# Summing y over the groups in DRAM with accumulating DMAs, in a grouped MLP with layer norm and projection

## The reference

```python
xr = x.reshape(Bx, Tx, 8, LATENT)
h = jnp.einsum('btel,elf->btef', xr, W1) + b1
h = jax.nn.gelu(h, approximate=False)
y = jnp.einsum('btef,efl->btel', h, W2) + b2
y = y.reshape(Bx, Tx, Dx)
eo = jax.nn.silu(emb) @ emb_W + emb_b
scale, shift = jnp.split(eo[:, None, :], 2, axis=-1)
hn = _layernorm(y, ln_g, ln_b) * (1.0 + scale) + shift
proj = jax.nn.silu(hn) @ out_W + out_b
return x + proj
```

## Time and profile before

| | |
|---|---|
| median of 3 runs | 706.13 us |
| lowest, highest | 706.08, 706.57 us |
| the profiled execution: span from first to last instruction | 704.2 us |
| PE busy | 700.5 us (99%) |
| DVE busy | 603.7 us (86%) |
| ACT busy | 469.3 us (67%) |
| POOL busy | 104.1 us (15%) |
| granted TensorE clock, mean over the span | 0.999 |

### The profile page before, as it was taken

One profiled execution on the slowest core, in us unless ns is written; L12 is line 12 of the kernel. 1 busy time (PEld: TensorE's weight loads), 2 busy tenths in 40 slices (PEclk: granted clock), 3 DMA queues, 4 the chain that ended last, 5 costly groups with the idle time before them and its releaser, 6 DMA issues.

```text
span 704.2 us, 8302 instructions
## 1 busy us (share of the span) xinstructions
PE 700.5 (99%) x3082; PEld 577.9 (82%) x3082; DVE 603.7 (86%) x725; ACT 469.3 (67%) x526; POOL 104.1 (15%) x68
## 2 busy tenths in 40 slices
PE   9999999999999999999999999999999999999998
PEld 6888888888888888888888888888888888888887
DVE  6888999999999989899887999999999978677512
ACT  7898888888878879888883456454656454555500
POOL 0000000000000011100121332423232432322100
PEclk9999999999999999999999999999999999999999
DMA  6766557344232531332789687887699877565531
GB/s 240 247 232 207 187 203 231 109 169 150 90 121 90 209 120 61 120 107 104 210 293 301 183 279 233 275 256 246 219 293 264 256 217 210 183 176 143 156 120 60
DMA packets 51880, 133.22 MB, mean 189 GB/s; under 512 B 4096, under 2 KB 25216, under 8 KB 49408
## 3 DMA queue, kind: packets, MB, share of 16 engines
q1 hardware_dynamic: 46944, 115.79, 46.9%
q0 software_dynamic: 4608, 16.78, 12.3%
q10 hardware_dynamic: 288, 0.13, 0.1%
HBM read 82.35 MB, written 33.55 MB: 165 GB/s over the span
## 4 chain that ended last, share of the span: by engine, by line
PE 99%; DMA 0%; ACT 0%; DVE 0%; issue 0%; DVEq 0%
PE psum L949 48%; PE psum L939 25%; PE psum L923 25%; PE psum L1001 2%; DMA wraw<-in_W 0%; PE psum L971 0%; ACT W L534 0%; DVE res L901 0%; DVEq L125 0%
## 5 line engine op out<-in xcount | busy, mean ns | idle before, releaser
L665 DVE TENSOR_TENSOR g_lo<-g_raw,g_hi 128x1024 fp32r<-128x1024 f32 x128 | 158.4, 1239 | 27.9 <-ACT g_hi L495 25.3
L489 ACT ACTIVATE g_raw<-psum,cols 128x1024 f32<-128x1024 f32 x128 | 142.9, 1116 | 34.1 <-PE psum L923 24.9
L949 PE MATMUL psum<-oW_hi,s_lo 128*128 128x512 f32 x496 | 152.7, 389 | 0.0
L949 PE MATMUL psum<-oW_hi,s_hi 128*128 128x512 f32 x496 | 152.7, 389 | 0.0
L949 PE MATMUL psum<-oW_lo,s_hi 128*128 128x512 f32 x496 | 152.6, 389 | 0.0
L939 PE MATMUL psum<-g_hi,W 128*128 128x512 f32 x512 | 136.8, 389 | 0.0
L923 PE MATMUL psum<-xT_hi,W 128*128 128x512 f32 x508 | 135.8, 389 | 0.0
L939 PEld LDWEIGHTS psum<-g_hi,W 128*128 128x128 f32 x512 | 96.1, 188 | 20.0
L923 PEld LDWEIGHTS psum<-xT_hi,W 128*128 128x128 f32 x508 | 95.3, 188 | 19.8
L949 PEld LDWEIGHTS psum<-oW_hi,s_hi 128*128 128x128 f32 x496 | 93.1, 188 | 19.4
L949 PEld LDWEIGHTS psum<-oW_hi,s_lo 128*128 128x128 f32 x496 | 93.1, 188 | 19.3
(11 more groups left out here) (77 smaller groups left out, 679.8 us busy)
## 6 DMA issues: line engine op xcount, KB each, us to landing
y_scratch<-y_stage SPq DMA_DIRECT2D x32, 512.0 KB, 3.1
yb<-y_scratch SPq DMA_DIRECT2D x16, 1024.0 KB, 4.8
res<-in_x SPq DMA_DIRECT2D x32, 512.0 KB, 6.1
res<-out_b_all POOLq DMA_DIRECT2D x32, 512.0 KB, 4.5
xT_raw<-in_xT SPq DMA_DIRECT2D x31, 512.0 KB, 4.3
out<-res SPq DMA_DIRECT2D x31, 512.0 KB, 4.1
tail_cols<-in_emb_T SPq DMA_DIRECT2D x24, 512.0 KB, 7.2
wraw<-in_out_W SPq DMA_DIRECT2D x16, 256.0 KB, 4.9
```

The lines of the kernel that those rows point to most:

```text
L489: nc.scalar.activation(g_raw[:, m % 2], ring(m), ACT.Gelu, bias=cols[:, R_B1 + k:R_B1 + k + 1]).then_inc(gelu_done, 1)
L665: nc.vector.tensor_tensor(g_lo[:, m % 2], g_raw[:, m % 2], g_hi[:, m % 2].bitcast(F32), ALU.subtract).then_inc(glo_done, 1)
L949: mm = nc.tensor.matmul(proj(q)[:, half], v[:, g, cut], w[:, g, half], start=(g == 0 and k == 0), stop=(g == G - 1 and k == 2))
```

## The change

A second DRAM tensor, `y_sum`, holds the sum of y over the groups. In the first stage the four items of group 0 are stored to it by an additional plain DMA on SP's queue, right behind the store to `y_scratch`. The other 28 items are added to it by an accumulating DMA on POOL's queue (`add_y`), each of 512 KB, 1 KB per row piece, from the same `y_stage` buffer. Each of these waits for the addition before it on the same tokens. `stage_y` now also waits until the buffer's additional DMA of two items earlier has landed. The mean loads 128 x 256 of `y_sum` into `mean_total` (`load_sum`, on SP's queue), and DVE's three additions per unit are gone, 48 instructions in all.

```diff
+    y_sum = nc.dram_tensor("y_sum", [NP, P, TP], F32, kind="Internal").ap()
...
+            def load_sum(p):
+                if p >= 1:
+                    sp.wait_ge(mean_done, p)
+                sp.dma_start(mean_total[:], y_sum[p]).then_inc(sum_landed, 16)
...
                     for p in range(2):
                         load_y(p)
+                    for s in range(2):
+                        sp.wait_ge(y_summed[s], 16 * len(range(NT + s, Y0_ITEM + 1, 2)))
+                if n == 22:
+                    sp.wait_ge(emb_dot, SUMS)
+                    load_sum(0)
+                if n == 24:
+                    load_sum(1)
+                if n == 26:
+                    load_sum(2)
...
                 sp.dma_start(y_scratch[PT * t:PT * t + PT, :, g].rearrange("h p t -> p h t"),
                              y_stage[:, n % 2].rearrange("p (h t) -> p h t", h=PT)).then_inc(y_stored[n % 2], 16)
+                if g == 0:
+                    sp.dma_start(y_sum[PT * t:PT * t + PT].rearrange("h p t -> p h t"),
+                                 y_stage[:, n % 2].rearrange("p (h t) -> p h t", h=PT)).then_inc(y_set[n % 2], 16)
...
             for s in range(2):
                 sp.wait_ge(y_stored[s], 16 * (N // 2))
+                sp.wait_ge(y_summed[s], 16 * ((N - NT) // 2))
             for q in range(QN):
+                if q % 2 == 0 and q // 2 + 3 < NP:
+                    load_sum(q // 2 + 3)
...
             def mean_of(p):
-                pool.wait_ge(mean_tree, 3 * p + 3)
+                pool.wait_ge(sum_landed, 16 * (p + 1))
...
-            mean_of(0)
-            mean_of(1)
-            var_of(0)
-            var_of(1)
+            def add_y(n):
+                g, t = ORDER[n]
+                last = ITEM_OF[g - 1, t]
+                if g == 1:
+                    pool.wait_ge(y_set[last % 2], 16 * (last // 2 + 1))
+                else:
+                    pool.wait_ge(y_summed[last % 2], 16 * ((last - NT) // 2 + 1))
+                pool.wait_ge(y_staged, n + 1)
+                pool.dma_start(y_sum[PT * t:PT * t + PT].rearrange("h p t -> p h t"),
+                               y_stage[:, n % 2].rearrange("p (h t) -> p h t", h=PT), accum_op=ALU.add
+                               ).then_inc(y_summed[n % 2], 16)
+
+            for n in range(NT, N):
+                add_y(n)
+                if n == 21:
+                    mean_of(0)
+                if n == 23:
+                    mean_of(1)
+                if n == 24:
+                    var_of(0)
+                if n == 26:
+                    mean_of(2)
+                if n == 28:
+                    var_of(1)
             pool.wait_ge(out_b_landed, 16)
             for q in range(2):
                 add_bias(q)
             for i in range(NP):
-                if i + 2 < NP:
-                    mean_of(i + 2)
                 if 2 * i + 2 < QN:
                     add_bias(2 * i + 2)
+                if i + 3 < NP:
+                    mean_of(i + 3)
...
                 if n >= 2:
                     act.wait_ge(y_stored[n % 2], 16 * (n // 2))
+                    if n - 2 < NT:
+                        act.wait_ge(y_set[n % 2], 16 * (n // 2))
+                    else:
+                        act.wait_ge(y_summed[n % 2], 16 * ((n - NT) // 2))
...
-                if ahead < NP:
-                    mean_sum_first(ahead)
-                    mean_sum_rest(ahead)
```

More of the change, by code:

```diff
@@ L189, in cond_ffn_program @@
         tail_cols = [at(f"tail_cols{k}", [P, K], R0 + o * KB) for k, o in enumerate((36, 40, 80, 84, 88, 92))]
-        mean_part1 = at("mean_part1", [P, HG, TP], R0 + 124 * KB)
         yb = (yb0, yb1, yb2)
@@ L237, in cond_ffn_program @@
         y_stored = [sem(f"y_stored{s}") for s in range(2)]
+        y_set = [sem(f"y_set{s}") for s in range(2)]
+        y_summed = [sem(f"y_summed{s}") for s in range(2)]
         y_landed = [sem(f"y_landed{s}") for s in range(3)]
-        mean_tree = sem("mean_tree")
+        sum_landed = sem("sum_landed")
         mean_done = sem("mean_done")
@@ L728, in modulation, with centre @@
                     nc.vector.tensor_scalar(half_c[:], mod_c[:, 0], 0.5, None, ALU.mult).then_inc(mod_step, 1)
-            def mean_part(p):
-                return mean_part1 if p == 1 else sq
-            def mean_sum_first(p):
-                if p == 1:
-                    dve.wait_ge(emb_dot, SUMS)
-                dve.wait_ge(y_landed[p % 3], 16 * (p // 3 + 1))
-                nc.vector.tensor_tensor(mean_part(p)[:, 0:4], yb[p % 3][:, 0:4], yb[p % 3][:, 4:8], ALU.add
-                                        ).then_inc(mean_tree, 1)
-            def mean_sum_rest(p):
-                part = mean_part(p)
-                dve.wait_ge(mean_tree, 3 * p + 1)
-                nc.vector.tensor_tensor(part[:, 0:2], part[:, 0:2], part[:, 2:4], ALU.add).then_inc(mean_tree, 1)
-                dve.wait_ge(mean_tree, 3 * p + 2)
-                if p >= 1:
-                    dve.wait_ge(mean_done, p)
-                nc.vector.tensor_tensor(mean_total[:], part[:, 0], part[:, 1], ALU.add).then_inc(mean_tree, 1)
-            def centre(p, h):
+            def centre(p, h):
+                dve.wait_ge(y_landed[p % 3], 16 * (p // 3 + 1))
                 dve.wait_ge(mean_done, p + 1)
@@ L817, in _ @@
                     modulation(0, EARLY, 0)
-                if (n, c) == (21, 1):
-                    mean_sum_first(0)
-                if (n, c) == (22, 1):
-                    mean_sum_rest(0)
-                if (n, c) == (22, 2):
-                    mean_sum_first(1)
                 if (n, c) == (23, 1):
@@ L827, in _ @@
                     centre(0, 1)
-                if (n, c) == (24, 1):
-                    mean_sum_rest(1)
                 if (n, c) == (24, 2):
```

## The result

The changed kernel took 720.09 us (median of 4 runs, 719.27 to 721.66) beside 706.33 us before (706.08 to 706.57): 1.0197 times as long, with a 95% interval of 1.0183 to 1.0212, so 13.8 us slower. The forecast was slower, 711.5 us: 5.4 us where 13.8 came.

What follows compares the result with a forecast made beforehand. PE was taken as the bound, never standing still, so less DVE work gains nothing. Waits of 1.5 + 1.1 + 0.5 + 2.3 = 5.4 us on 706.13 gave 711.5 us; range 705.9 to 722, the case's own 707.2 to 716.

Steps and rivals of the forecast that it cites:

- term 0: Removing DVE's three additions per unit, some 37 us over 16 units, gains nothing, since PE is not waiting.
- The turn's path: Turn of the stages: bias additions behind add_y(31) land late, delaying finish(0), embedding columns and finish(1), so PE waits.
- Stores ahead of x: Items 0 to 3: second stores delay x; PE waits 1.5 us after item 2 and 1.1 after item 3.
- The 2 MB piece: Where a 2 MB piece comes too, engine work reaches into the next item; PE waits 0.5 us (0 to 0.7).
- Steady items: First stage: x goes before the addition, whose 3 us fit in the rest of the 10.88 us item; no loss.
- POOL's statistics: POOL's waits on mean and variance stand behind additions, but these are ready within the item: cost nothing.
- rival (b): Additions get ahead of x in 28 items, PE waits 1.4 to 1.9 us each: 746 to 759 us; chance 0.13.
- the case that I gave 0.05: Partial case of additions getting ahead of x: 716 to 725 us; chance 0.05.
- the 2.5 to 3 us that I had worked out: How much later x would land in 28 items if the additions got ahead of it.
- the signs that I had named: Among them: x lands near 4.0 to 4.5 us from item 14 on; first bias addition lands near 369.
- 6 us or more: Sign that the forecast is wrong: x lands this long after its issue in steady items.
- The turn: Turn of the stages: finish(0) moves by 5.4 us and PE waits 2.3 us (0 to 4.5).

Runs made afterwards that it cites:

- e7: The kernel before, with DVE's three additions per unit cut to one of two groups: 706.31 us, ratio 0.9997.
- e1: The changed kernel with group 0's four plain stores to y_sum issued behind the load of x and the next weights: 715.18 us, ratio 1.0141.
- e2: The changed kernel with the first two bias additions issued behind the addition of item 29, ahead of items 30 and 31: 716.76 us, ratio 1.0153.
- e14: The changed kernel with POOL's all-reduce of the mean of unit 2 moved ahead of the addition of item 26: 719.36 us, ratio 1.0187.
- e10: The changed kernel with the edits of e1 and e2 together, the additions of y issued at once: 712.05 us, ratio 1.0077.
- e6: The changed kernel with plain copies in place of the 28 accumulating DMAs, leaving the summing out: 714.56 us, ratio 1.0112.
- e5: The changed kernel with y_sum laid out for 4 KB pieces, 128 per addition instead of 512: 726.43 us, ratio 1.0281.
- e12: e10, but SP issues each load of x before it waits for y and stores it: 708.43 us, ratio 1.0029.
- e4: The changed kernel with the edits of e1, e2 and e3 together: 716.43 us, ratio 1.0133.
- e3: The changed kernel with each accumulating DMA issued only when the x loaded beside it has landed: 723.6 us, ratio 1.025.

## Why the prediction was right and wrong

**Right: the sign, and that DVE's work is worth nothing.** "So nothing that takes work off DVE can gain" was term 0; e7 measured 0.9997. The turn's path was also the right one (bias late, `finish(0)`, embedding columns, `finish(1)`, PE), and so was the place of the early loss, the x behind item 2's stores; moving each (e1, e2) took its loss away.

**Stores ahead of x: forecast 1.5 + 1.1 = 2.6, measured 5.3.** After item 2 PE waited 2.6 us against 1.5, inside the bounds of 0.4 to 3.1. After item 3 it waited nothing against 1.1: the wait before had made PE itself late. Items 0 and 1, costed at nothing, gave 1.0: the x behind item 0's two stores took 6.65 us. What the sum had no term for is the clock, 1.7 us behind this one wait. The scatter is large here: e14, in which nothing of this part is changed, loses 3.5 by item 6, with no single wait over 0.8 us. So the nearness of 1.5 and 2.6 is partly luck.

**The 2 MB piece: forecast 0.5, measured 1.1** in items 6 to 10, above the bound of 0.7. No experiment took the piece away; that it is the cause rests on the place, and e1, e2 and e10, which leave this part as it is, lost nothing from item 7 to 10.

**Steady items: forecast 0, measured 4.7 (items 23 to 31).** This is the step that failed: "By that x goes first, and the 3 us lie in the rest of the item". The first half held: the bias DMA of rows 10 had indeed come last (its first packet 5.1 us after the issue, 1.5 as a rule), and in after 81% of a load of x starts before the addition's first packet. What did not follow is that an x that goes first is undisturbed, and that was put at nothing without a row that shows it. Its packets take 274 ns instead of 186, and it lands 5.6 us after its issue in this stretch instead of 4.1. Between 70 and 230 us x takes 0.9 us more (5.3 against 4.4 in the middle), and from item 11 to 22 PE loses next to nothing. Between 230 and 340 us it takes 1.5 more and PE loses 4.7 us, in steps of 1.3, 1.4, 1.2 and 0.5 at items 25, 26, 28 and 30. That fits a number that stood in the rival, "It decides from an x that lands over 1.1 us later in steady items", but 1.1 is no sharp point: in e6 an x 0.8 us later went with 1.7 lost. The step of 1.2 is where the all-reduce stands beside `g_lo`. For this there was no term either: I had put POOL's statistics down at "nothing" since they are ready within the item, and did not ask what DVE does beside them.

So rival (b) had the late x and neither its cause nor its size, and the case that I gave 0.05, "716 to 725", holds the result. By the Trainium skill's rule that I weighed ("DMA: Bandwidth & Descriptors", section "Queues, rings and completion order"), engines going round-robin between queue rows, x would be slowed where both have packets to send. The trace has that for the last fifth of x, and e5 for longer, up to 8.5 us to landing; but most of x was slow with nothing of the addition to take turns with, and the 2.5 to 3 us that I had worked out did not come. Of the signs that I had named, x "near 4.0 to 4.5 us" failed (5.6), and so did a first bias addition near 369 (384); "6 us or more" was reached by single loads only (6.3 at most).

**The turn: forecast 2.3 (0 to 4.5), measured 4.4.** `finish(0)` came 8.6 us later against PE's own lag, where I had 5.4: `add_y(31)` took 13.8 us, not the 3 us of engine time and 2 us of way that I had put ahead of the bias. PE's wait was 2.8, the rest the clock again. So a shift of 5.8 us was hidden, more than the 4.4 to 5.4 of the working; with those, a shift of 8.6 would have made PE wait 3.2 to 4.2.

**The sum.** Of the 10.3 us missed in the profiled execution (15.7 less 5.4), the clock is 3.2, items 23 to 31 are 4.7, and the rest, 2.4, are waits of which each was forecast within about a factor of two.

**Open.** What slows the packets of x between POOL's issue and the addition's first packet is not known; it came with a copy as with an addition, and with 128 packets as with 512. Nor is it known when PE's clock falls behind a wait: in e1 PE stood 3.0 us at the turn, and the clock stayed at 1.00. A version faster than before didn't come out, and e7 says why: PE never waits for what the change saves.

## What to carry to other kernels

Work on an engine that nobody waits for costs nothing (e7), while the DMAs that replace it delayed a load with 0.85 us to spare. So before moving a sum into DMAs, find the load with the least slack and ask what is issued ahead of it, what is in flight beside it, and how much it can stretch: here 0.9 us more cost next to nothing, and 1.5 us more cost PE 3 to 5. Going first doesn't protect it. If the traffic must be there, issue the tight load earlier (e12: from 13.8 down to about 2 us with the same bytes, the two bias additions moved as well). And when costing a wait of PE of two us or more, look for a trace that shows the clock behind one.

## What was not expected of the hardware

- Two waits of PE of 2.6 and 2.8 us were each followed by a granted clock of 0.50 for 2.6 to 2.9 us, which cost 1.7 and 1.5 us. It fell too behind waits of 2.4 us in e4 (0.54 over 3 us), 2.2 in e14 and 2.0 in e5. It stayed at 1.00 behind waits of 1.9 us (e3 at 258 us, e5 at 404) and less, and also behind the one of 3.0 us in e1.
- An accumulating DMA of 512 KB from SBUF to DRAM on POOL's queue, in 1 KB pieces, landed 8.2 to 11.0 us after its issue with x beside it (150 to 330 us) and 5.9 to 7.5 as a plain copy on the same queue (e6), while a plain store of the same y on SP's queue took 3.1. At 128 packets each, adding took 8.3 us (e5, 328 ns a packet) and copying 6.2 (e6, 159 ns). In the landing the adding is the smaller part; in the kernel's time it is the larger, 5.5 us of 8.1.
- A load of x on SP's queue, issued just before a DMA on POOL's queue and served first, had its packets slowed from 186 to 274 ns, before that DMA's first packet.
- 4 KB pieces in place of 1 KB left the addition's landing nearly as it was (8.3 us against 8.5 in the middle), and x too (5.4), and made the kernel 6 us slower.
- An all-reduce of POOL beside a two-input instruction of DVE can stretch that, from 1.22 us to between 1.3 and 3.3, already in the kernel before (1.51 and 2.10); in other overlaps it stayed at 1.23.
